# One chip, eight cores, a whole transformer layer: the softmax's transposed copies move from ScalarE to VectorE, and the score matmuls are put in another order

## What is computed

```python
kv = rmsnorm(x @ w_dkv, g_kv)
k_nope = (kv @ w_uknope)...   v = (kv @ w_uv)...
k_rope = rope(x @ w_ukrope)
q = rmsnorm(x @ w_dq, g_q) @ w_uq        # 16 heads x (128 + 64)
scores = q_nope . k_nope + q_rope . k_rope, scaled, causal mask
out = softmax(scores) @ v;  x + out @ w_o
```

## Time and profile before

| | us |
|---|---|
| median of the 2 runs shown | 5731.62 |
| the runs | 5660.69 and 5802.55 |
| the profiled execution | 5666.73 |
| its span, first to last instruction, slowest core | 5665.2 |
| spans of the eight cores | 5634.2 to 5665.2 |
| attention steps (block pc, with projections) in it | from 426 to 2543 |

### The profile page before, as it was taken

The page is one execution under the profiler, slowest core; times in us unless marked ns, Lnnn a source line. Parts: engine busy times, 40 slices in busy tenths (PEclk is TensorE's granted clock), DMA queues, the critical chain, the costliest instruction groups (busy, mean ns, idle before and its releaser), DMA issues. The chain is left out here.

```text
span 5665.2 us, 59103 instructions; the slowest of 8 cores (5634.2 to 5665.2 us)
## 1 busy us (share of the span) xinstructions
PE 4083.6 (72%) x20688; PEld 1947.1 (34%) x20688; DVE 1841.5 (33%) x3067; ACT 1547.2 (27%) x2098; POOL 287.4 (5%) x509
## 2 busy tenths in 40 slices
PE   2936775767577757763965777777888888798879
PEld 1413332333233323331433433343333333343334
DVE  4453334333533353333135656560000000001000
ACT  5203332333233323330026666660000000000000
POOL 0000000000000000000000111111000100010001
PEclk9965555555555555555976788788999999999999
DMA  6012222222222222223447878874443444444344
GB/s 180 1 24 78 77 69 60 73 73 69 67 69 72 67 69 67 73 64 75 147 150 230 262 256 266 264 233 157 147 130 128 162 146 134 147 148 140 130 154 154
DMA packets 270288, 710.16 MB, mean 125 GB/s; under 512 B 27762, under 2 KB 83058, under 8 KB 247988
## 3 DMA queue, kind: packets, MB, share of 16 engines
q1 hardware_dynamic: 198628, 462.56, 25.2%
q0 software_dynamic: 71376, 243.83, 14.9%
HBM read 619.25 MB, written 102.76 MB: 127 GB/s over the span
## 5 line engine op out<-in xcount | busy, mean ns | idle before, releaser
L1317 PE MATMUL e1s_px<-BB,e1s_t 128*128 128x512 bf16 x5632 | 1310.9, 392 | 163.3 <-DMA e1s_t<-w2qT 124.7
L1317 PEld LDWEIGHTS e1s_px<-BB,e1s_t 128*128 128x128 bf16 x5632 | 554.1, 101 | 883.4 <-issue 305.4
L1436 PE MATMUL e2s_pu<-e2s_w,h_sb 128*128 128x512 bf16 x2816 | 625.8, 386 | 100.3 <-DMA e2s_w<-w3qT 79.0
L944 ACT COPY PT_sb<-ps_pt 128x1024 bf16<-128x1024 bf16 (+7 forms) x384 | 293.0, 763 | 916.2 <-PE ps_pt L659 916.2
L1280 DVE TENSOR_TENSOR h_sb<-e1s_sg,e1s_px 128x512 bf16<-128x512 f32 x176 | 121.0, 687 | 1247.3 <-PE e1s_px L1317 1247.3
L887 DVE TENSOR_REDUCE stat<-ps_sc 128x1 f32<-128x128 f32 (+15 forms) x256 | 330.3, 1290 | 521.4 <-PE ps_sc L785 520.5
L670 PE MATMUL ps_o<-v_sb,PT_sb 128*128 128x128 bf16 x2176 | 272.7, 308 | 251.7 <-ACT PT_sb L944 251.7
L659 PE MATMUL ps_pt<-idn_sb,P_sb 128*128 128x128 bf16 x2176 | 303.2, 310 | 185.8 <-ACT PT_sb L944 159.7
L1436 PEld LDWEIGHTS e2s_pu<-e2s_w,h_sb 128*128 128x128 bf16 x2816 | 278.6, 99 | 447.5 <-issue 126.6
L773 PE MATMUL ps_sc<-kn_sb,qn_sb 128*128 128x512 bf16 (+3 forms) x640 | 343.8, 537 | 104.0 <-ACT P_sb L932 90.3
L932 ACT ACTIVATE P_sb<-ps_sc,stat 128x128 bf16<-128x128 f32 (+15 forms) x256 | 296.6, 1158 | 442.3 <-DVE stat L887 442.0
(11 more groups left out here) (161 smaller groups left out, 3292.0 us busy)
## 6 DMA issues: line engine op xcount, KB each, us to landing
gb<-w SPq DMA_DIRECT2D x264, 256.0 KB, 2.9
dump<-w SPq DMA_DIRECT2D x264, 256.0 KB, 2.9
e1s_w<-w SPq DMA_DIRECT2D x66, 1024.0 KB, 8.5
e1s_w<-w POOLq DMA_DIRECT2D x66, 1024.0 KB, 8.5
e1s_t<-w1qT SPq DMA_DIRECT2D x132, 512.0 KB, 3.3
e1s_t<-w2qT POOLq DMA_DIRECT2D x132, 512.0 KB, 3.6
e2s_w<-w3qT POOLq DMA_DIRECT2D x176, 256.0 KB, 3.0
e2s_w<-w3qT SPq DMA_DIRECT2D x176, 256.0 KB, 3.1
```

The lines of the kernel that those rows point to most:

```text
L944: e.copy(PT_sb[:, b0 * 128:(b0 + bl) * 128], ps_pt[:, 0:bl * 128]).then_inc(s_pte, 1)
L1317: ins = e.matmul(dst[:, 0:512], wqT[i % 2][:, kc * 128:(kc + 1) * 128], BB3[:, kc, sg * SG:(sg + 1) * SG], start=(kc == 0), stop=(kc == KC ...
L1436: ins = e.matmul(pu[tl * 2 + sub][:, 0:512], h_sb[:, c * 512 + tl * 128: c * 512 + (tl + 1) * 128], w3s[buf(r, c)][:, sub * 512: (sub + 1) ...
```

## The change

Four edits, all in block pc.
1. The score matmuls of a step are put in another order: first the 128-row matmuls of all chunks, then the 64-row ones of all chunks, then the mask. Their number, operands and results stay.
2. The copies from ps_pt to PT_sb are taken out of ACT's program.
3. They are put into DVE's `vflush`, ahead of its wait for the exp and the reciprocal, as `tensor_copy`. DVE therefore does them after the maximum of the next step.
4. DVE calls `vflush` also ahead of a "pack", if a step is pending, as PE did before.

```diff
--- before.py
+++ after.py
@@ -769,24 +769,24 @@
                             nck = (klen + 511) // 512
                             for ck in range(nck):
                                 nn = min(512, klen - ck * 512)
-                                diag = (ck == nck - 1)
                                 e.matmul(ps_sc[:, off + ck * 512:
                                                off + ck * 512 + nn],
                                          qn_sb[:, qi * 128:(qi + 1) * 128],
                                          kn_sb[:, ck * 512:ck * 512 + nn],
                                          start=True, stop=False)
+                            for ck in range(nck):
+                                nn = min(512, klen - ck * 512)
+                                diag = (ck == nck - 1)
                                 ins = e.matmul(
                                     ps_sc[:, off + ck * 512:
                                           off + ck * 512 + nn],
                                     qr_sb[:, qi * 128:(qi + 1) * 128],
                                     KR[:, ck * 512:ck * 512 + nn],
                                     start=False, stop=not diag)
-                                if diag:
-                                    ins = e.matmul(
-                                        ps_sc[:, off + klen - 128:
-                                              off + klen],
-                                        idn_sb[:, :], mask_sb[:, :],
-                                        start=False, stop=True)
+                            ins = e.matmul(
+                                ps_sc[:, off + klen - 128:off + klen],
+                                idn_sb[:, :], mask_sb[:, :],
+                                start=False, stop=True)
                             ins.then_inc(s_sc, 1)
                             n["sc"] += 1; n["mx"] += 1; n["ex"] += 1
                             if tpend[0] is not None:
@@ -803,6 +803,13 @@
                     def vflush(e):
                         kp, qp, ip = vpend[0]
                         vpend[0] = None
+                        for (b0, bl) in _tp_batches(qp):
+                            n["tp"] += 1
+                            e.wait_ge(s_tp, n["tp"])
+                            e.tensor_copy(PT_sb[:, b0 * 128:(b0 + bl) * 128],
+                                          ps_pt[:, 0:bl * 128]
+                                          ).then_inc(s_pte, 1)
+                            n["pte"] += 1
                         e.wait_ge(s_ex, kp + 1)
                         e.reciprocal(lcol[:, 2 + kp % 2:3 + kp % 2],
                                      lcol[:, kp % 2:kp % 2 + 1])
@@ -823,6 +830,8 @@
                             pass
                         elif kind == "pack":
                             g, n2 = step[1], step[2]
+                            if vpend[0] is not None:
+                                vflush(e)
                             n["pk"] += 1
                             e.wait_ge(s_pk, n["pk"])
                             eo = n2 % 2
@@ -889,8 +898,6 @@
                                          axis=AX.X,
                                          negate=True).then_inc(s_mx, 1)
                             n["mx"] += 1; n["ex"] += 1
-                            nb = len(_tp_batches(qi))
-                            n["tp"] += nb; n["pte"] += nb
                             if vpend[0] is not None:
                                 vflush(e)
                             vpend[0] = (k_g, qi, idx)
@@ -938,12 +945,6 @@
                                                         k_g % 2 + 1]
                                          ).then_inc(s_ex, 1)
                             n["ex"] += 1
-                            for (b0, bl) in _tp_batches(qi):
-                                n["tp"] += 1
-                                e.wait_ge(s_tp, n["tp"])
-                                e.copy(PT_sb[:, b0 * 128:(b0 + bl) * 128],
-                                       ps_pt[:, 0:bl * 128]).then_inc(s_pte, 1)
-                                n["pte"] += 1
                             n["pv"] += 1; n["oe"] += 1
 
         tap_block("otm", BB[:, :])
```

## The result

| | before | after |
|---|---|---|
| profiled execution's span, us | 5665.2 | 5487.6 |
| median of all executions, us | 5675.17 (10) | 5511.51 (11) |
| ratio after / before | 1 | 0.9691, interval 0.9667 to 0.9714 |
| attention stage, first to last scaled output (L812, L819), us | 2115.6 | 1938.2 |

The account below looks back on a forecast made before the run. The prediction took a chain of waits in the attention stage as the bound, with exp behind copies on ACT. Copies -42, order -83 and clock -35 sum to -160 us, from 5666.7 to 5507 us, range 5400 to 5600.

Parts of the forecast that it names:

- What bounds it: Attention stage: a chain of waits, no engine full; from step 8 exp stands behind copies in ACT's queue, releasing the scores.
- Copies to DVE: Attention steps: exp leaves the chain, copies queue behind the next maximum; 2.6 us gained a head, 42 us over sixteen heads.
- The price of a copy: DVE copies of transposed batches from PSUM: 0.681 us for 1024 columns, about 0.41 for 512.
- the end of a head: From the mask of step 15 to the next projection: 12.65 us instead of 13.41, gain 0.76.
- The loss in steps 2 to 6: Small steps, where the maximum now precedes the copy: 0.29 us lost in step 4, 1.5 over the five steps.
- Order of the matmuls: Score matmuls: weight loads are exposed where row count changes; 48 fewer a head at 0.108 us, 83 us in all.
- Clock: Late attention steps: unbroken product and scores raise the clock; 35 us put in the sum, 50 at most.
- the transposes' share: Steps 12 to 15: second transposes at the high clock level save about 0.3 of 0.7 us a step.
- A: Rival, score matmuls: 64-row weight loads stay exposed, -42 - 41 and no clock gain, 5584 us; chance 0.17.
- B: Rival, score matmuls: no weight loads hidden, exposure is a matter of the score tiles, 5625 us; chance 0.09.
- C: Rival, copies: DVE becomes the bound at the f32 cast's price, +146, leaving -14; chance 0.06 with all its kind.
- D: Rival, attention: clock stays high through steps 12 to 15, -147 more, 5360 us; chance 0.08.

Follow-up runs that it names:

- pad_inter: Kernel before, score order kept, with KR and qr_sb padded with zeros from 64 to 128 rows: ratio 0.9697, stage 165.8 us shorter.
- order_only: Kernel before with only the new order of the score matmuls: ratio 0.9817 to the kernel before, attention stage 89.3 us shorter.
- copy_only: Changed kernel with the interleaved score order put back, so only the copies move to DVE: ratio 0.9872 to the kernel before, stage 68.7 us shorter.
- split_pad: Changed kernel with copies divided between ACT and DVE, and KR and qr_sb zero-padded to 128 rows: ratio 0.9277 to the kernel before.

## Why the prediction was right, point by point

- **What bounds it.** Right. The exp in ACT's queue set steps 7 to 15; doubling ACT's reduction cost 127 us before, 101 of it in steps 7 to 14, and 12 after.
- **Copies to DVE, -42.** The mechanism held and the size was low: 68.7 by itself. The terms mis-sized are two links that stand in every step: from the maximum to the copy, put at nothing where 0.08 is to be taken off, and from the product to the next scores, 0.05 too long. Together with smaller ones they come to 0.11 a step, 25 us. The price of a copy (0.682 and 0.420 us measured, 0.681 and 0.41 taken) and the end of a head (12.60, 12.65 forecast) were right. The loss in steps 2 to 6 was too high for 4 (0.15 measured, 0.29 forecast) and too low for 3 (0.43): the sum had no term for what stands ahead of the maximum on DVE, in some heads a reduction with a late load.
- **Order of the matmuls, -83.** 89.3 measured by itself, 0.113 a load where the sum had 0.108. The choice to treat 64-row behind 64-row like 128 behind 128 was a guess, and pad_inter and order_only bear it out. The sentence of the Trainium skill (TensorE: Matmul & The Clock Gate, The mechanism) by which loads hide only behind other row groups does not hold here: with equal rows they hide (0.42 to 0.43 us from start to start), and at a change from 128 to 64 rows they do not (0.54). The same section also names a background weight buffer as a way to load ahead; no run here shows what is used.
- **Clock, -35.** The halves give -89.3 and -68.7, together -158.0; both at once give -177.4. The 19 us that only both together bring (22 in the medians) are the term forecast at 35, overestimated but there. The ratios are too wide to show it; the clock's record does. In steps 8 to 15 the 2.4 GHz level held for 14 us in order_only, 12 in copy_only and 150 in the changed kernel. Of these 30 fell in scores, 1 in order_only and 8 in copy_only, and there each saves about one us, since four score matmuls take 0.92 us at that level and 1.81 below it. That it needs the product right before unbroken scores is what the forecast said. What failed is the transposes' share, 0.3 of the 0.7 us put on each late step: the six of step 14's second batch took 0.80 us on average, as in copy_only. The place was not only the late steps either: step 9 had 7 of the 30 us.
- **Sum.** -160 forecast, -177 measured in the stage: one term 27 too small, one 6 too small, one 16 too large. Errors of opposite sign flattered the total, and that it came within 10% is in part luck.
- **The rivals.** A and B fell to order_only, C to the price of the copies. D was not reached: the clock stayed at 0.62 in the stage, and even split_pad, which takes away more waits, has 0.73.

## What to carry to other kernels

Look at what stands in an engine's queue in front of the instruction on the chain, not at how busy the engine is: here an unrelated 0.63 us reduction ahead of an exp cost 91 us on the slowest core, 82 in the medians, and moving it needed no other engine. Divide evacuations over the engines by who is idle when the data is ready, rather than giving them all to the faster one. Between matmuls of 128 and of 64 rows a weight load was exposed; grouping them by shape took most of these back, padding the smaller with zeros all of them, and with padding the granted clock rose too. When an instruction is moved behind another in a queue, look at what that one waits for as well: the copy now also stands behind a reduction whose DMA can be late, which never held it up before.

## What was not expected of the hardware

- Zeros in 64 added rows made the kernel faster by 3% (0.9697, interval 0.9558 to 0.9836): a 64-row matmul of 512 columns takes the same 0.43 us as a 128-row one, and each change of the row count costs 0.113 us. The granted clock of the stage was 0.64 with the zeros and 0.57 with grouped 64-row matmuls; whether the rows or the last gaps do that is open.
- DVE, reading bf16 from PSUM, is faster than ACT: 0.68 us against 1.01 for 1024 columns, also while ACT reads the scores (1123.45 and 1123.63 above).
- Where DVE's next instruction waits for nothing, it starts 0.08 us before the recorded end of the one ahead (maximum to copy, 0.081 to 0.086 in 240 cases). Chains summed from durations come out long by that much at each such place.
